# Layer 0's row steps in other slots, the MLP as one program, and more low probabilities on VectorE

## What is computed

```python
def _L0_xattn_ref(query, key, value, ...):        # layer 0: E = 512, H = 16 heads of 32
    qn, kn, vn = (_layer_norm(t, ln1_g, ln1_b) for t in (query, key, value))
    Q, K, V = qn @ wq + bq, kn @ wk + bk, vn @ wv + bv     # per head
    attn = softmax(Q K^T / sqrt(HD))
    out = (attn @ V).reshape(B, Sq, E) @ wo + bo
    x = residual + out
    y = _layer_norm(x, ln2_g, ln2_b)
    y = gelu(y @ w1 + b1, approximate=False) @ w2 + b2
    return x + y

def _L1_xattn_ref(q, k, v, Wq, Wk, Wv, Wfc, gamma, beta):   # layer 1: 16 heads of 64
    weights = softmax((q @ Wq) / sqrt(DK) (k @ Wk)^T + const)
    out = (weights @ (v @ Wv)) @ Wfc + q
    return layer_norm(out) * gamma + beta
```

## Time and profile before

| what | us |
|---|---|
| median of 3 runs | 1459.75 |
| lowest and highest of them | 1459.64, 1460.61 |
| the profiled execution's own time | 1459.83 |
| its span (first to last instruction) | 1458.1 |
| step U-1 of attention 0, about | 413 to 482.8 |
| closing step U and step U+1 | 482.8 to 528.2 |
| mlp_up on PE | 529.86 to 604.7 |
| rows_w2 on PE | 607.22 to 684.8 |
| first matmul of attention 1 | 686.54 |

### The profile page before, as it was taken

One profiled execution on the slowest core, in us unless ns is written; L12 is line 12 of the kernel. 1 busy time (PEld: TensorE's weight loads), 2 busy tenths in 40 slices (PEclk: granted clock), 3 DMA queues, 4 the chain that ended last, 5 costly groups with the idle time before them and its releaser, 6 DMA issues.

```text
span 1458.1 us, 31567 instructions
## 1 busy us (share of the span) xinstructions
PE 1376.1 (94%) x12865; PEld 875.9 (60%) x12865; DVE 877.7 (60%) x1576; ACT 685.7 (47%) x1322; POOL 452.4 (31%) x493
## 2 busy tenths in 40 slices
PE   6989999999998779999999999999999999999997
PEld 4556666666664545444556666666666666666665
DVE  6768778878877758434435454455554455545565
ACT  3547666766754645221224444444444444444432
POOL 3125566666665731200001111112111111121123
PEclk9999999999999889999999999999999999999999
DMA  8226443444443044132333334123333321423321
GB/s 260 66 62 169 124 128 83 131 122 140 109 134 97 9 152 133 58 109 104 123 80 70 103 70 111 41 51 101 71 103 71 92 60 40 112 65 97 96 72 39
DMA packets 117533, 140.56 MB, mean 96 GB/s; under 512 B 49789, under 2 KB 91789, under 8 KB 115341
## 3 DMA queue, kind: packets, MB, share of 16 engines
q1 hardware_dynamic: 116201, 136.28, 34.4%
q10 hardware_dynamic: 1188, 2.27, 0.5%
HBM read 63.15 MB, written 21.35 MB: 58 GB/s over the span
## 4 chain that ended last, share of the span: by engine, by line
PE 47%; DVE 3%; issue 1%; ACT 1%; POOL 0%; POOLq 0%; ACTq 0%; DVEq 0%
PE attn_p_proj L1101 17%; PE attn_p_proj L1096 14%; PE attn_p_max L1123 3%; PE attn_p_sc L1318 2%; PE attn_p_sc L1154 2%; PE attn_p_sc L1153 2%; PE attn_p_pv L1182 1%; PE attn_p_proj L1245 1%; PE attn_p_pv L1181 1%; PE attn_p_pv L1183 1%; DVE attn_nmax L1696 1%; PE attn_p_max L1245 1%; DVE attn_knat L1729 1%; ACT attn_probs L1464 1%; ACT attn_knat L1493 0%
## 5 line engine op out<-in xcount | busy, mean ns | idle before, releaser
L807 POOL TENSOR_TENSOR attn_probs<-kernel_w_first,attn_probs 128x400 f16<-128x400 f32 x96 | 90.6, 944 | 674.3 <-ACT attn_probs L1464 674.3
L1696 DVE TENSOR_REDUCE attn_nmax<-attn_p_max 100x1 f32<-100x722 f32 x250 | 226.0, 904 | 118.9 <-PE attn_p_max L1123 116.4
L1101 PE MATMUL attn_p_proj<-kv_w_v,attn_ctxT 128*128 128x512 f16 (+1 forms) x1152 | 264.3, 379 | 0.0
L1454 ACT ACTIVATE kernel_w_first<-attn_p_sc,attn_score_bias 128x400 f32<-128x400 f32 x192 | 113.5, 591 | 307.9 <-PE attn_p_sc L1154 307.9
L1096 PE MATMUL attn_p_proj<-attn_ctxT,kv_w_k 128*128 128x361 f16 x1536 | 249.1, 317 | 4.1 <-DVE attn_knat L1729 3.5
L807 POOL TENSOR_TENSOR attn_probs<-attn_p,attn_probs 128x400 f16<-128x400 f32 x186 | 202.6, 1094 | 155.4 <-ACT attn_probs L1464 149.9
L1096 PEld LDWEIGHTS attn_p_proj<-attn_ctxT,kv_w_k 128*128 128x128 f16 x1536 | 144.6, 97 | 88.6 <-DVE attn_knat L1729 9.7
L1101 PEld LDWEIGHTS attn_p_proj<-kv_w_v,attn_ctxT 128*128 128x128 f16 (+1 forms) x1152 | 110.4, 101 | 111.0
L1454 ACT ACTIVATE attn_p<-attn_p_sc 128x400 f32<-128x400 f32 x192 | 96.2, 501 | 147.2 <-PE attn_p_sc L1150 143.2
L1101 PE MATMUL attn_p_proj<-l_w_v,attn_ctxT 128*128 128x512 f16 (+1 forms) x576 | 133.4, 382 | 1.0 <-DVE attn_vbuf L1735 0.9
L1096 PE MATMUL attn_p_proj<-attn_ctxT,kernel_w_first 128*128 128x361 f16 x768 | 129.2, 319 | 0.0
(11 more groups left out here) (259 smaller groups left out, 2589.3 us busy)
## 6 DMA issues: line engine op xcount, KB each, us to landing
kv_w<-attn_knat SPq DMA_DIRECT2D x128, 180.5 KB, 3.5
attn_kstack<-attn_knat SPq DMA_DIRECT2D x192, 90.2 KB, 2.2
ctx_turned<-attn_ctxT SPq DMA_DIRECT2D x8, 1444.0 KB, 8.1
attn_ctxT<-ctx_turned SPq DMA_DIRECT2D x8, 1444.0 KB, 8.7
attn_kstack_b<-attn_knat SPq DMA_DIRECT2D x64, 180.5 KB, 3.6
attn_c<-in_ctx_dram SPq DMA_DIRECT2D x35, 256.0 KB, 3.7
kv_w_v<-in_L_xattn_w_dram SPq DMA_DIRECT2D x7, 1024.0 KB, 5.5
q_parts<-attn_probs SPq DMA_DIRECT2D x16, 200.0 KB, 2.4
```

The source lines that it names most:

```text
L807: eng.tensor_tensor(probs[:r, g % 2, 1, t, :HG * SQ], p32[:r, t % 3, :], probs[:r, g % 2, 0, t, :HG * SQ], ALU.subtract).then_inc(p_lo_mad ...
L1101: last = pe.matmul(bank[:r, :], ctxT[:, cpar, ca, k, P * t:P * t + r], w_v[:, wa, k, c0:c0 + E], **flags)
L1454: act.activation(p32[:r, t % 3, :], p_sc[:r, t % 2, :HG * SQ], ACT.Exp, bias=bias_col[:r, 0:1] if score_bias else 0.0).then_inc(exp_made, 1)
L1696: dve.tensor_reduce(nmax[:SQ, hh:hh + 1], max_banks(u, g, hh)[:SQ, :, :HALF], AX.XY, ALU.max, negate=True).then_inc(max_made, 1)
```

## The change

Three parts.

**1. Row steps.** In layer 0 the row tiles' steps get other slots. The bias goes one or two slots earlier. The statistics are split off from `row_sum` as `row_stat` and go one slot later, behind that slot's maximum; pow then has offset +4, centring +5, final +6, high part +7, low part +8, turn +10, copy +11. T = 4 keeps sum and statistics in the first slot and gets offsets of its own; its turn goes from among the last P·V products to behind them, and into a bank of its own (`p_max`, half 0), as does the second part of the last batch's output transposes (`p_max`, half 1), so that neither waits for `misc`. The low part of the last output's first three heads' groups (`last_out_lo(0)`) goes from slot 6 to slot 4.

**2. Low probabilities.** `shared_lo` also lists t = 1, 3, 5 of group 1: VectorE makes nine of the closing step's low parts and GpSimd fifteen. GpSimd's `normalise` of one old group moves from slot 23 to slot 18 of that step.

**3. One MLP program.** `mlp_up` and `rows_stage` become `mlp`. There is one block and one barrier fewer: the w2 products follow the up-products on PE, and the bank of four accumulators is shared. The next layer's weights are loaded into two rooms (w_first, w_qo) once 20 of the 32 uses are done. Each row tile's transposes come one row tile later rather than two, and VectorE's order is sum, copy of the tile before, low part, low part of the weight.

```diff
--- before.py
+++ after.py
-def rows_stage(nc, name, ident16, res_d, w=None, lhs=(), res=None, bias=None, norm=None, keep=None, store=None, xT=None,
...
-def mlp_up(nc, ident16, x_d, x1_d, xT, w_o, w_first, w, m_tiles, x1, b2_row, bias_col, scale, outT, vectors, b2_d, split, room, split_rooms):
+def mlp(nc, ident16, x_d, x1_d, xT, w_o, w_first, w, w2, m_tiles, x1, b2_row, bias_col, scale, hT, vectors, b2_d, store, split, room, split_rooms,
+        next_split, next_rooms):
...
-            sp.wait_ge(x1_loaded, 16)
-            sp.wait_ge(b2_loaded, 16)
+            sp.wait_ge(acc_ready, m_tiles + 4)
+            for n in range(2):
+                next_weights.load(sp, n)
+            for T, r in enumerate(RROWS):
+                next_weights.load(sp, 2 + T)
+                sp.wait_ge(down_summed, T + 1)
+                sp.dma_start(store[ROW0[T]:ROW0[T] + r, :], x1[:r, T]).then_inc(row_stored, 16)
+            sp.wait_ge(row_stored, 16 * RT)
...
+            for i in range(RT + 1):
+                if i < RT:
+                    r0, r = ROW0[i], RROWS[i]
+                    if i == 0:
+                        pe.wait_ge(weight_split.lo_made, len(weight_split.jobs))
+                    pe.wait_ge(lo_made, m_tiles if r0 + r <= QHALF else 2 * m_tiles)
+                    pe.wait_ge(*((made, 2 * m_tiles - 3 + i) if i < 4 else (down_summed, i - 3)))
+                    n = 0
+                    for k in range(m_tiles):
+                        for a, b in PARTS:
+                            last = pe.matmul(acc[:r, i % 4, :], hT[:, a, k, r0:r0 + r], w2[:, b, k, :], start=(n == 0), stop=(n == 3 * m_tiles - 1))
+                            n += 1
+                    last.then_inc(down_ready, 1)
+                T = i - 1
+                if T >= 0:
+                    r = RROWS[T]
+                    pe.wait_ge(row_lo_made, T + 1)
+                    if T >= 2:
+                        pe.wait_ge(row_copied, T - 1)
+                    for a, part in enumerate((hi, lo)):
+                        for k in range(ET):
+                            last = pe.transpose(row_tr[T % 2][:, a, k, :r], part[:r, T % 3, k * P:(k + 1) * P], ident16[:r, :r])
+                    last.then_inc(row_turned, 1)
...
+            def down_copy(T):
+                r = RROWS[T]
+                dve.wait_ge(row_turned, T + 1)
+                dve.tensor_copy(xT[:, :, :, ROW0[T]:ROW0[T] + r], row_tr[T % 2][:, :, :, :r]).then_inc(row_copied, 1)
+
+            for T, r in enumerate(RROWS):
+                dve.wait_ge(down_ready, T + 1)
+                dve.wait_ge(down_biased, T + 1)
+                dve.scalar_tensor_tensor(x1[:r, T], acc[:r, T % 4, :], 1.0 / WS, x1[:r, T], ALU.mult, ALU.add).then_inc(down_summed, 1)
+                if T >= 1:
+                    down_copy(T - 1)
+                dve.wait_ge(row_hi_made, T + 1)
+                dve.tensor_tensor(lo[:r, T % 3], x1[:r, T], hi[:r, T % 3], ALU.subtract).then_inc(row_lo_made, 1)
+                next_weights.lo(dve, T)
+            down_copy(RT - 1)
...
+            pool.wait_ge(acc_ready, 2 * m_tiles)
+            pool.wait_ge(x1_loaded, 16)
+            pool.wait_ge(b2_loaded, 16)
+            for T, r in enumerate(RROWS):
+                if T >= EARLY:
+                    pool.wait_ge(centred, nth(T))
+                pool.tensor_tensor(x1[:r, T], x1[:r, T], b2_row[:r], ALU.add).then_inc(down_biased, 1)
...
-        self.row_bias = [3, 8, 13, 20]
+        self.row_bias = [3, 7, 12, 18]
         self.row_base = [3, 9, 15, 21, 42]
         self.last_acc = {16: 0, 17: 1, 18: 2, 19: 3}
         self.last_bias_t = 17
-        self.last_row = {2: 1, 3: 2, 4: 6, 5: 6}
+        self.last_row = {2: 1, 3: 1, 4: 3, 5: 3, 6: 6, 7: 6, 8: 7, 10: 12, 11: 13}
         self.row_place = [4, 9, 13, 17, 18]
-        self.row_acc, self.row_sum, self.row_pow, self.row_centre, self.row_final, self.row_hi, self.row_lo, self.row_turn = 0, 2, 3, 3, 4, 5, 7, 9
-        self.shared_lo = {(last, g, t) for g in (2, 3) for t in (1, 3, 5)} if layer == 0 else set()
+        self.row_acc, self.row_sum, self.row_stat, self.row_pow, self.row_centre = 0, 2, 3, 4, 5
+        self.row_final, self.row_hi, self.row_lo, self.row_turn, self.row_copy = 6, 7, 8, 10, 11
+        self.shared_lo = {(last, g, t) for g in (1, 2, 3) for t in (1, 3, 5)} if layer == 0 else set()
...
-            if outs and j == self.out_t:
-                uses.append(("out", 1 if layer0_end else 0))
+            if outs and j == self.out_t and not layer0_end:
+                uses.append(("out", 0))
...
+        last16 = [p_max[:, i, :].bitcast(F16) for i in range(2)]
...
-                misc_wait(s, ("out", part))
+                if part == 0:
+                    misc_wait(s, ("out", 0))
                 for a in range(2):
                     for k in ks:
                         o = (a * ET + k) * P
-                        last = pe.transpose(misc16[:, o:o + SQ], oparts[:SQ, a, k * P:(k + 1) * P], ident16[:SQ, :SQ])
-                last.then_inc(misc_ready, 1)
+                        last = pe.transpose((misc16, last16[1])[part][:, o:o + SQ], oparts[:SQ, a, k * P:(k + 1) * P], ident16[:SQ, :SQ])
+                last.then_inc(last_out_turned if part else misc_ready, 1)
 
...
-                misc_wait(s, ("row", T))
+                if T < EARLY - 1:
+                    misc_wait(s, ("row", T))
                 for a in range(2):
                     for k in range(ET):
                         o = (a * ET + k) * P
-                        last = pe.transpose(misc16[:, o:o + r], cparts[:r, T % 2, a, k * P:(k + 1) * P], ident16[:r, :r])
-                last.then_inc(misc_ready, 1)
+                        last = pe.transpose((misc16 if T < EARLY - 1 else last16[0])[:, o:o + r], cparts[:r, T % 2, a, k * P:(k + 1) * P], ident16[:r, :r])
+                last.then_inc(misc_ready if T < EARLY - 1 else last_row_turned, 1)
 
...
-                    if sl.row_tile(s, j, sl.row_turn + 1) is not None:
-                        row_copy(sl.row_tile(s, j, sl.row_turn + 1))
+                    if sl.row_tile(s, j, sl.row_copy) is not None:
+                        row_copy(sl.row_tile(s, j, sl.row_copy))
...
-                if (g, t) == (2, 1):
+                if (g, t) == (1, 1):
                     dve.wait_ge(p_lo_made[1], lo_count(u, g - 1, KT - 1))
...
                 dve.scalar_tensor_tensor(mid[T][:r], p_proj[:r, row_use(T) % 2, :], 1.0 / WS, mid[T][:r], ALU.mult, ALU.add).then_inc(proj_freed, 1)
+
+            def row_stat(T):
+                r = RROWS[T]
                 dve.wait_ge(proj_freed, row_use(T) + 1)
                 dve.bn_stats(stats[:r, T % 2, :], mid[T][:r]).then_inc(mid_stats_made, 1)
                 dve.wait_ge(mid_stats_made, T + 1)
...
-                        if j == 6:
+                        if j == 4:
                             last_out_lo(0)
...
+                    if sl.row_tile(s, j, sl.row_stat) not in (None, EARLY - 1):
+                        row_stat(sl.row_tile(s, j, sl.row_stat))
                     if sl.row_tile(s, j, sl.row_sum) is not None:
                         row_sum(sl.row_tile(s, j, sl.row_sum))
+                    if sl.row_tile(s, j, sl.row_stat) == EARLY - 1:
+                        row_stat(EARLY - 1)
...
-                    if layer == 0 and s == U and j == NSLOT - 1:
+                    if layer == 0 and s == U and j == KT * (NG - 1):
                         normalise(s - 1, 1)
...
-                mlp_up(nc, ident16, x_rows, x1_d, x_parts, w_qo, w_first, w1p, FT, x1, b2_row, b1_col, 1.0 / WS, hT,
...
-                rows_stage(nc, "rows_w2", ident16, None, w=w2p, lhs=[hT], res=x1, bias=b2_row, keep=x1, store=x2_d, xT=x_parts,
...
+                mlp(nc, ident16, x_rows, x1_d, x_parts, w_qo, w_first, w1p, w2p, FT, x1, b2_row, b1_col, 1.0 / WS, hT,
+                    vectors=(bo, ln2_g, ln2_b), b2_d=b2, store=x2_d,
+                    split=part_jobs(columns(w1), w1p)[1:] + tile_jobs(w2, w2p, ET), room=w_k[:],
+                    split_rooms=[as_f32(staging[:, 2 * ET * E * i:2 * ET * E * (i + 1)]) for i in range(2)],
+                    next_split=part_jobs(columns(wq1), w_q) + part_jobs(columns(wk1), w_k) + part_jobs(columns(wv1), w_v),
```

224 lines of the change are left out of this document (38 added, 186 removed).

## The result

| | median us | lowest to highest | runs |
|---|---|---|---|
| before | 1459.7 | 1457.97 to 1460.61 | 4 |
| after | 1450.15 | 1449.24 to 1452.21 | 4 |

The ratio is 0.9938, 95% interval 0.9924 to 0.9953: 9.0 us less, between 6.9 and 11.1 (the two medians lie 9.6 apart). Forecast were 1448.2 and 11.7 us less. The profiled execution took 1449.99, its span is 1448.2.

The account below looks back on a forecast made before the run. PE was taken to bound the kernel (busy 94%), so time is won only where it idles or runs at the lower clock. 3.5 + 5.2 + 2.56 + 0.4 = 11.66 off 1459.83 gave 1448.2 us, range 1444.0 to 1453.5 (82%).

Parts of the forecast that it names:

- step U-1: Layer 0 attention, 413 to 482.8 us: moved row steps remove PE waits, 3.5 us, bounds 1.9 and 5.3.
- closing steps: Steps U and U+1, 482.8 to 528.2 us: moved low parts and row tile 4's steps give 5.2, bounds 2.5 and 6.3.
- w2 boundary: Between up- and w2 products: PE's wait at the barrier, 2.56 us, goes in full.
- end of w2: Tile 5's transposes come before the last sum's low part, so one wait goes: 0.4 us, bounds 0 and 0.5.
- Row tile 0's statistics: Step U-1: 1.03 us of VectorE ahead of the maximum at 430.46; moving them a slot later gives 0.7.
- the new one on misc: Step U-1, slot 14: output transposes wait for ScalarE's copy of tile 0's turn; 1.3 us taken off, bounds 0 and 1.65.
- Row tiles 2 and 3: Step U-1: the 1.33 wait goes, the 0.92 wait grows by up to 0.5; net 1.0, bounds 0.6 and 1.6.
- the last P·V set: Closing steps: the P·V products at 520.51 come 3.5 us earlier, at about 517.0.
- the low parts at the P·V products of group 1: Closing steps: GpSimd loses three low parts, 2.8 us in all, to VectorE; 2.0 of it kept at these products.
- Row tile 4's turn: End of closing steps: with all 48 P·V products in one run 2.1 us are won, 1.7 of it kept.
- The price of the shared port: Closing steps: VectorE and GpSimd slow each other; at a whole 0.92 per moved low part, 2.4 instead of 5.2.
- VectorE binds: Rival, 28%: moved low parts hold up maxima; closing steps give 2.4, step U-1 1.9, total 1452.6 us.

Follow-up runs that it names:

- e10: Kernel after with turn and copy of row tiles 0 to 3 one slot earlier (offsets 9 and 10): 1447.72 us, ratio 0.9932.
- e3: Kernel after with the low parts of group 1 on GpSimd again and normalise in slot 23 again: 1452.45 us, ratio 0.9967.
- e8: Kernel after with VectorE's copy of the turned row maxima ahead of the low part, not behind it: 1449.78 us, ratio 0.9936.
- e4: Kernel after with the steps of row tiles 0 to 3 in their old slots, row tile 4 as in after: 1453.31 us, ratio 0.997.
- e6: Kernel after with GpSimd's normalise of the old group in slot 23 of the closing step again: 1449.81 us, ratio 0.9935.
- after again: The kernel after, unchanged, run and traced a second time: 1450.82 us, ratio 0.9939 to before.

## Why the prediction was right, and by which of its steps

The sign and the range were right. The size was 2.7 too large, with 11.7 just above the interval's 11.1, and of the terms the largest one failed:

| term | forecast | measured (trace) |
|---|---|---|
| step U-1 | 3.5 | 4.4 |
| closing steps | 5.2 | 0.4 |
| w2 boundary | 2.56 | 2.7 |
| end of w2 | 0.4 | -0.2 |
| sum | 11.7 | 7.3 |

**Step U-1.** Row tile 0's statistics gave 1.2 by slot 7, and 0.35 of it was lost again in slot 7, where the maximum behind them is now late (PE waits 0.16 for it at 434.62): 0.8 for the 0.7 that the forecast took. The tile's second wait went in full, 1.4 for 0.9, and so did the first of row tile 1, 1.5 for 1.05 by slot 13. From slot 13 to 16 the waits of 1.13 and, not counted in the forecast, 0.72 are gone and the new one on misc has come, 1.65 by PE's row and 1.1 by e10 where it is taken away: together nothing (12.30 and 12.28). Row tiles 2 and 3 gave 0.65 and not 1.0; the evacuation behind the high part is 1.44 for 0.92, the 0.5 that was taken for it.

**Closing steps.** This is the step that failed: 0.4 for 5.2. Up to the last P·V set, where the forecast had 3.5 less, the closing step is 0.85 to 0.95 us longer than before (38.57 for 37.72, 38.31 for 37.36); behind it 1.4 is won for 1.7. Three things are behind this.

First, the sum held 2.0 for the low parts at the P·V products of group 1, with VectorE's own cost counted as lying within it by its free share, 3.92 busy of 7.00. The gain came, 2.0 from slot 12 to 17 (e3), but 1.0 or more was lost from slot 4 to 12, and those P·V products came later and not earlier. The share had been read in the wrong place: the window from 505 to 512 begins at the P·V products of group 1, and the moved low parts stand in slots 7, 9 and 11 ahead of it. In the two windows ahead, which hold slots 3 to 7 and 8 to 14 of the kernel before, VectorE was busy 6.47 of 7.00 and 7.28 of 10.00 us (columns as in the earlier trace rows), and so had 8% and 27% of its time free, not 44%:

```profile
488.00:495.00 7.00, 6.74 (x85) 5.89 (x85) 6.47 (x12) 3.83 (x9) 6.76 (x8) 0.58 0.15 3
495.00:505.00 10.00, 5.51 (x89) 3.71 (x88) 7.28 (x12) 8.27 (x18) 8.34 (x12) 0.96 0.01 2
```

Besides, VectorE stands at a low part waiting for ScalarE, with PE's maximum behind it. This mechanism was in the forecast, at 0.4; in the second trace of after it is two waits of 0.94 and 0.98. That it makes the loss is argued from these rows: e8, which takes one of the two away, did not settle what it is worth.

Second, the row steps of tiles 2 and 3 were priced in step U-1 only. Moved later, they fall into the closing step, where VectorE was fullest, and cost 1.4 to 1.9 there (e4). By the table at e4, up to slot 17 the low parts alone give 1.35 and the new row steps alone cost 0.5; together they cost 0.3, where the sum would be a gain of 0.85.

Third, the 3.5 at the last P·V set held 1.5 beyond the 2.0, for row tile 4's steps, with no row behind it, and none of it was found. GpSimd's normalise, moved to slot 18, was not priced: it delays the scores of slot 23 by 0.7 (PE's 1.20 at 513.06) and shortens the way behind the last P·V product by 1.8, a gain of 0.9 (e6). Without this unpriced gain the closing steps would have been longer than before, 47.21 for 46.71.

Row tile 4's turn is right: 1.4 for 1.7.

**Two marks that came out right by luck.** The last P·V set starts at 517.00 and the first up-product at 525.00, as the forecast had them (517.0 and 524.7). But the forecast took these marks from the closing steps alone; with its own 3.5 for step U-1 they should have been 513.5 and 521.2. The 517.00 is made of an opening 1.7 later, 6.0 less in step U-1 (1.6 of it the clock) and 0.9 lost behind it.

**The price of the shared port.** Had each moved low part cost a whole one of GpSimd's, 2.8 us would have gone. In ten executions with these low parts on VectorE the first two took 0.56 to 0.67, about what they take alone; the third, in slot 11, took 1.05 in after, 1.42 in after again and up to 1.50, which reaches the 1.4 that the prediction had named as a sign of being wrong. What it meets is GpSimd's output low part. In after again:

```profile
499.71 1.15 POOL L2022 TENSOR_TENSOR attn_oparts<-attn_o,attn_oparts 100x512 f16<-100x512 f32 x1
500.84 1.26 POOL L690 TENSOR_TENSOR attn_probs<-attn_p,attn_probs 128x400 f16<-128x400 f32 x1
```

VectorE's, begun at 499.87, ends at 501.29, 0.43 after the first of these, and the second ends 0.81 after VectorE's, at 502.10. The rows look as if one were served after the other to the full; the cost is smaller than the bound because only one in three meets another operation: 0.5 to 0.9 on VectorE and 0.3 on GpSimd.

**The rival "VectorE binds"** had the cause right and the place in the closing step, and 1452.6 for it, 7.3 less. The intervals above add up to the same 7.3, but otherwise made: 4.4 in step U-1 where this rival had 1.9, and 0.4 in the closing steps where it had 2.4.

**What the trace does not account for.** 9.0 by the runs (6.9 to 11.1), 7.3 by the intervals: the 1.7 between them lie inside the interval and were not traced to a cause. The spans of the two pairs of traces differ by 9.9 and by 5.8. What of that is not in the 7.3 lies, beside the 1.6 of clock in step U-1 of the first pair, in stretches that the forecast left as they were: the opening up to step U-1 (1.65 and 1.05 longer in after), the up-products (0.1 and 0.7 longer) and attention 1 (2.6 and 0.1 shorter). The granted clock is one candidate: mean 0.983 in before's profile, 0.986 to 0.987 in the runs of after. That the total came out within 2.7 us of the forecast is in part luck: step U-1 gave 0.9 more than its term, and this 1.7 came on top, against 4.8 missing in the closing steps.

## What to carry over

Read the free share of an engine in the very slots that the moved work will stand in, and not in a window near them. Even there it says nothing of an instruction that waits: before moving work to an engine that works in order, look at what will be queued behind it when its input is late, and price that wait at the gap between the engine's turn and the input, per instance. Where two parts of a change put work on the same engine in the same slots, price them together. Price a step that is moved later in the stage where it now falls, not where it left. Where two traces execute the same matmuls, compare the times between the same ones: where the granted clock was alike such intervals repeated to 0.02 us here, while the 95% intervals of whole runs reached 1.4 to 2.4 us to each side.

## What the runs showed of the hardware

The granted clock of TensorE fell to its lower level, 1.2 GHz, in stretches that differ from one execution to the next with the same code. Windows of before, first and second execution, then of after, first and second, at the same places (columns as in the earlier trace rows; the granted clock is the third number from the end):

```profile
456.00:460.00 4.00, 4.00 (x26) 2.10 (x25) 3.33 (x6) 1.35 (x3) 2.95 (x5) 0.57 0.54 124
```

```profile
456.00:460.00 4.00, 3.82 (x32) 2.19 (x33) 3.73 (x7) 1.73 (x4) 3.34 (x5) 1.00 0.51 118
```

```profile
679.00:686.00 7.00, 6.75 (x40) 3.94 (x41) 4.50 (x14) 1.47 (x3) 0.00 (x0) 1.00 0.84 315
```

```profile
679.00:686.00 7.00, 6.95 (x29) 3.56 (x30) 3.60 (x13) 1.01 (x2) 0.00 (x0) 0.69 0.87 332
```

The first pair is the 1.64 us by which slots 13 to 16 differ (13.94 and 12.30); the second is the start of attention 1, where the first trace of after ran all at full clock and the second did not, and where before had 0.58 from 686 to 693. By the time of attention 1's last query product the first had gained 2.6 on before and the second 0.5. Behind that product all four traces take the same 736.6 us. A gain of that size in one trace of each kernel is no gain of the change. What decides between such executions was not found.
